# Rank-48 adapter products in a block of FFN, attention and FFN: three fp32r partial products instead of one float32 product

## The reference, cut to what is computed

```python
x = x + 0.5 * ffn(layernorm(x))        # first FFN
x = x + attention(layernorm(x))        # 32 heads, causal, 2 x 1024 rows
x = x + 0.5 * ffn(layernorm(x))        # second FFN, same weights

def ffn(x):                            # x: (2, 1024, 1024), all float32
    y = einsum('bsd,od->bso', x, weight) + bias
    seg = searchsorted(lora_start_indices, arange(2), side='right') - 1
    adapter_idx = clip(seg - 1, 0, 2)  # which of 3 adapters the batch row uses
    A, Bw = lora_A[adapter_idx], lora_B[adapter_idx]     # rank 16
    lo = (x @ A.T) @ Bw.T
    return y + where(seg > 0, lo, 0)
```

## Time and profile before

| | |
|---|---|
| median of 3 runs | 1962.72 us (1962.16 to 1965.12) |
| the profiled execution | 1964.07 us, of which 1962.1 us span |
| mean granted TensorE clock | 0.974 of 2.4 GHz |
| TensorE matmul busy | 1819.1 us, 93% |
| VectorE, ScalarE, GpSimd busy | 1230.6, 997.6, 870.1 us |
| FFN 1 | from the start to about 246 us |

### The profile page before, as it was taken

How to read it: one execution, slowest core, us unless ns; L and a number is a source line. 1 busy time by engine, 2 the same in 40 slices (tenths; PEclk the granted TensorE clock), 3 DMA queues, 4 the chain that set the end, 5 groups by cost and what they waited for, 6 DMA issues and landing times. The chain is left out here.

```text
span 1962.1 us, 44377 instructions
## 1 busy us (share of the span) xinstructions
PE 1819.1 (93%) x15472; PEld 1423.7 (73%) x15472; DVE 1230.6 (63%) x2653; ACT 997.6 (51%) x2135; POOL 870.1 (44%) x641
## 2 busy tenths in 40 slices
PE   6999968689999999999999999997699999979999
PEld 4678767667777777777777777775488888857887
DVE  5555356378889889888898888887421121125553
ACT  2211055478888888888887888885410010012110
POOL 2231110268777787787877877873000000004311
PEclk9999989899999999999999999999799999989999
DMA  6442152402221221211212212211742223224321
GB/s 224 167 167 91 60 150 71 107 23 70 65 77 50 71 77 55 83 60 55 83 60 72 66 49 83 66 67 56 261 134 88 86 96 117 65 107 158 132 86 65
DMA packets 111695, 182.45 MB, mean 93 GB/s; under 512 B 27472, under 2 KB 64464, under 8 KB 109584
## 3 DMA queue, kind: packets, MB, share of 16 engines
q1 hardware_dynamic: 111632, 181.61, 28.5%
HBM read 122.06 MB, written 59.51 MB: 93 GB/s over the span
## 5 line engine op out<-in xcount | busy, mean ns | idle before, releaser
L940 PE MATMUL psS<-keyT,q 128*128 128x512 f32 (+2 forms) x2304 | 474.3, 351 | 32.7 <-POOL q L1145 25.3
L940 PEld LDWEIGHTS psS<-keyT,q 128*128 128x128 f32 x2304 | 381.9, 190 | 127.6 <-DVE negmax L1071 41.4
L1021 ACT ACTIVATE prob<-prob,negmax 128x640 f32<-128x640 f32 (+7 forms) x512 | 391.9, 767 | 78.7 <-DVE negmax L1071 76.4
L1081 DVE STREAM_TRANSPOSE pT<-prob 128x640 f32<-128x640 f32 (+7 forms) x512 | 380.2, 762 | 66.3 <-PE psV L957 63.3
L1071 DVE CUSTOM_DVE_ANT_0 prob<-psS,mask 128x640 f32<-128x640 f32 (+7 forms) x512 | 371.9, 742 | 40.0 <-PE psS L940 26.3
L413 PE MATMUL f_psy<-f_weff,f_xT 128*128 128x512 f32 x1344 | 313.9, 393 | 0.0
L1307 PE MATMUL o_psy<-o_w,o_o 128*128 128x512 f32 x1344 | 304.8, 389 | 0.0
L1136 POOL TENSOR_TENSOR pT<-pT,cosT 64x512 f32<-64x512 f32 x128 | 164.6, 1286 | 302.6 <-ACT pT L1006 288.5
L1307 PEld LDWEIGHTS o_psy<-o_w,o_o 128*128 128x128 f32 x1344 | 252.3, 188 | 52.3
L413 PEld LDWEIGHTS f_psy<-f_weff,f_xT 128*128 128x128 f32 x1344 | 250.8, 188 | 54.0 <-issue 1.7
L957 PE MATMUL psV<-pT,val 32*64 32x512 f32 (+3 forms) x8192 | 264.8, 407 | 6.6 <-DVE pT L1081 6.2
(11 more groups left out here) (99 smaller groups left out, 1882.3 us busy)
## 6 DMA issues: line engine op xcount, KB each, us to landing
wo<-in_wo SPq DMA_DIRECT2D x16, 1024.0 KB, 5.6
pT<-row_scales SPq DMA_DIRECT2D x128, 128.0 KB, 2.8
oT<-pT SPq DMA_DIRECT2D x64, 256.0 KB, 2.4
o_in<-oT SPq DMA_DIRECT2D x32, 512.0 KB, 5.2
f_xt<-in_x SPq DMA_DIRECT2D x16, 512.0 KB, 4.1
f_w_in<-in_w SPq DMA_DIRECT2D x16, 512.0 KB, 6.9
w_sum<-f_w_in SPq DMA_DIRECT2D x16, 512.0 KB, 5.1
x<-f_xo SPq DMA_DIRECT2D x16, 512.0 KB, 3.0
```

The lines of the kernel that those rows point to most:

```text
L940: ins = nc.tensor.matmul(psS[:, slot, start + x0:start + x1], q[:, e, a, t * P:(t + 1) * P], k.keyT[:, m, b * S + x0:b * S + x1], start=(i ...
L1021: nc.scalar.activation(row, row, ACT.Exp, bias=negmax[:, n % 8:n % 8 + 1], scale=-1.0, accum_out=rowsum[:, column(n, s):column(n, s) + 1]) ...
L1081: nc.vector.transpose(pT[:, n % 2, t, 0:width], prob[:, n % RING, 0:width]).then_inc(turned, 1)
```

## The change

The adapters' A and B are packed to 48 rows and padded to `PACKED` = 64, and loaded twice, into partitions 0 to 63 and 64 to 127. `lora_a` and `lora_b` now lie in `xo`. ScalarE rounds both copies to fp32r (`gated[:, 0]` for A, `b_hi` for B), ahead of the first `root_of`. GpSimd computes `b_lo`, the rest of B, before its first piece. VectorE replaces the upper 64 rows of A by their rest (`adapters_lo`) before gate_of(0). `gate_of` writes fp32r over 128 rows. A piece's half is then two fp32r matmuls: 128 rows against `b_hi` (A hi B hi + A lo B hi), and 64 rows against `b_lo` (A hi B lo). `wanted` becomes an input of 128 x 1 that is loaded instead of set by GpSimd. GpSimd's first two `add_bias` wait for both gates, since `xo` holds the adapters until then.

```diff
+            lora_a, lora_b = xo[:, 0, :], xo[:, 1, :]
+            b_lo = c.sb("lora_b_lo", [PACKED, D], F32R)
+            b_hi = c.sb("lora_b_hi", [P, D], F32R)
+            gated = c.sb("gated", [P, B, D], F32R)
@@ sync
-                sp.dma_start(starts[:], ...to_broadcast([GATED, STARTS])).then_inc(starts_in, 16)
-                sp.dma_start(lora_a[:], a_d[:, :]).then_inc(a_in, 16)
-                sp.dma_start(lora_b[:], b_d[:, :]).then_inc(b_in, 16)
+                sp.dma_start(starts[:], ...to_broadcast([P, STARTS])).then_inc(starts_in, 16)
+                sp.dma_start(wanted[:], wanted_d[:, :]).then_inc(starts_in, 16)
+                for rows in (slice(0, PACKED), slice(PACKED, P)):
+                    sp.dma_start(lora_a[rows, :], a_d[:, :]).then_inc(a_in, 16)
+                    sp.dma_start(lora_b[rows, :], b_d[:, :]).then_inc(b_in, 16)
@@ gpsimd
+                elif w_d is not None:
+                    pool.wait_ge(gate, B)
                 nc.gpsimd.tensor_tensor(xo[:, j, :], f.xt[:, j, :], bias_half[:], ALU.add)
...
-                for a in range(ADAPTERS):
-                    nc.gpsimd.memset(wanted[32 * a:32 * a + 32, :], float(a + 2)).then_inc(numbered, 1)
+                pool.wait_ge(b_split, 1)
+                nc.gpsimd.tensor_tensor(b_lo[:], lora_b[0:PACKED, :], b_hi[0:PACKED, :].bitcast(F32),
+                                        ALU.subtract).then_inc(b_rest, 1)
+                pool.wait_ge(b_rest, 1)
             pieces_low([0])
@@ scalar
+                act.wait_ge(a_in, 32)
+                nc.scalar.activation(gated[:, 0, :], lora_a, ACT.Copy).then_inc(a_split, 1)
+                act.wait_ge(b_in, 32)
+                nc.scalar.activation(b_hi[:], lora_b, ACT.Copy).then_inc(b_split, 1)
             f.root_of(nc, act, k.eps_ln[:], 0, 0)
@@ tensor
-                    pe.wait_ge(b_in, 16)
+                    pe.wait_ge(b_split, 1)
+                    pe.wait_ge(b_rest, 1)
...
-                    ins = nc.tensor.matmul(ps_w[:, half, :], gated[:, i // DT, (i % DT) * P:(i % DT + 1) * P],
-                                           lora_b[:, half * BANK:(half + 1) * BANK], start=True, stop=True)
+                    nc.tensor.matmul(ps_w[:, half, :], gated[:, i // DT, x], b_hi[:, y], start=True, stop=False)
+                    ins = nc.tensor.matmul(ps_w[:, half, :], gated[0:PACKED, i // DT, x], b_lo[:, y], start=False, stop=True)
@@ vector
+            def adapters_lo():
+                dve.wait_ge(a_split, 1)
+                nc.vector.tensor_tensor(lora_a[PACKED:P, :], lora_a[PACKED:P, :],
+                                        gated[PACKED:P, 0, :].bitcast(F32), ALU.subtract).then_inc(a_rest, 1)
+                dve.wait_ge(a_rest, 1)
...
             f.normalise(nc, dve, 0, 0)
             if w_d is not None:
+                adapters_lo()
                 gate_of(0)
             make_pieces([0])
```

More of the change, by code:

```diff
@@ L33 @@
 STARTS = 4
-GATED = 32 * ADAPTERS
+PACKED = 64
 QT = S // P
@@ L214, in ffn_phase @@
             ps_w = c.ps(tag + "ps_w", [P, 2, BANK])
[L215 to L223, removed]
+            lora_a, lora_b = xo[:, 0, :], xo[:, 1, :]
+            b_lo = c.sb("lora_b_lo", [PACKED, D], F32R)
+            b_hi = c.sb("lora_b_hi", [P, D], F32R)
+            gated = c.sb("gated", [P, B, D], F32R)
+            starts = c.sb("starts", [P, STARTS], I32)
+            startf = c.sb("startf", [P, STARTS])
+            hit = c.sb("hit", [P, B, STARTS])
+            count = c.sb("count", [P, B])
+            wanted = c.sb("wanted", [P, 1])
+            chosen = c.sb("chosen", [P, B])
             starts_in, a_in, b_in = c.sem("starts_in"), c.sem("lora_a_in"), c.sem("lora_b_in")
-            numbered, chain, gate = c.sem("numbered"), c.sem("chain"), c.sem("gate")
+            chain, gate = c.sem("chain"), c.sem("gate")
+            a_split, b_split, a_rest, b_rest = c.sem("lora_a_hi"), c.sem("lora_b_hi"), c.sem("lora_a_lo"), c.sem("lora_b_lo")
         bias_in, halved = c.sem(tag + "bias_in"), c.sem(tag + "halved")
@@ L270, in _ @@
             if w_d is not None:
-                a_d, b_d, starts_d = adapters
-                sp.dma_start(starts[:], starts_d.rearrange("(a n) -> a n", a=1).to_broadcast([GATED, STARTS])).then_inc(starts_in, 16)
-                sp.dma_start(lora_a[:], a_d[:, :]).then_inc(a_in, 16)
-                sp.dma_start(lora_b[:], b_d[:, :]).then_inc(b_in, 16)
+                a_d, b_d, starts_d, wanted_d = adapters
+                sp.dma_start(starts[:], starts_d.rearrange("(a n) -> a n", a=1).to_broadcast([P, STARTS])).then_inc(starts_in, 16)
+                sp.dma_start(wanted[:], wanted_d[:, :]).then_inc(starts_in, 16)
+                for rows in (slice(0, PACKED), slice(PACKED, P)):
+                    sp.dma_start(lora_a[rows, :], a_d[:, :]).then_inc(a_in, 16)
+                    sp.dma_start(lora_b[rows, :], b_d[:, :]).then_inc(b_in, 16)
             load_w(0)
@@ L341, in pieces_hi @@
                     nc.scalar.activation(weff[:, i // DT, HI, i % DT, :], w_in[:, i % SLOTS, :], ACT.Copy).then_inc(w_hi, 1)
+            if w_d is not None:
+                act.wait_ge(a_in, 32)
+                nc.scalar.activation(gated[:, 0, :], lora_a, ACT.Copy).then_inc(a_split, 1)
+                act.wait_ge(b_in, 32)
+                nc.scalar.activation(b_hi[:], lora_b, ACT.Copy).then_inc(b_split, 1)
             f.root_of(nc, act, k.eps_ln[:], 0, 0)
@@ L373, in outer_products @@
                 for half in range(2):
-                    ins = nc.tensor.matmul(ps_w[:, half, :], gated[:, i // DT, (i % DT) * P:(i % DT + 1) * P],
-                                           lora_b[:, half * BANK:(half + 1) * BANK], start=True, stop=True)
+                    x, y = slice((i % DT) * P, (i % DT + 1) * P), slice(half * BANK, (half + 1) * BANK)
+                    nc.tensor.matmul(ps_w[:, half, :], gated[:, i // DT, x], b_hi[:, y], start=True, stop=False)
+                    ins = nc.tensor.matmul(ps_w[:, half, :], gated[0:PACKED, i // DT, x], b_lo[:, y], start=False, stop=True)
                 ins.then_inc(outer, 1)
@@ L437, in link @@
                     dve.wait_ge(chain, next(links))
-                dve.wait_ge(starts_in, 16)
-                dve.wait_ge(numbered, ADAPTERS)
+                dve.wait_ge(starts_in, 32)
                 link(nc.vector.tensor_copy(startf[:], starts[:]))
@@ L445, in choose @@
                     link(nc.vector.tensor_scalar(chosen[:, b:b + 1], count[:, b:b + 1], wanted[:, 0:1], None, ALU.is_equal))
+            def adapters_lo():
[3 more added lines that the diff above has]
+                dve.wait_ge(a_rest, 1)
             def gate_of(b):
-                dve.wait_ge(a_in, 16)
-                nc.vector.tensor_scalar(gated[:, b, :], lora_a[:], chosen[:, b:b + 1], None, ALU.mult).then_inc(gate, 1)
+                nc.vector.tensor_scalar(gated[:, b, :], lora_a, chosen[:, b:b + 1], None, ALU.mult).then_inc(gate, 1)
             def results(n, j):
@@ L1315, in output_steps, with macaron_block @@
     steady(eng, step, NT, 1, 1, start=0)
-def macaron_block(nc, x, wa, lnw, wn, wpe, wv, wo, cos, sin, cosT, sinT, w, bias, lora_a, lora_b, starts, out):
+def macaron_block(nc, x, wa, lnw, wn, wpe, wv, wo, cos, sin, cosT, sinT, w, bias, lora_a, lora_b, starts, wanted, out):
     x1_d = nc.dram_tensor("x1", (T, D), F32).ap()
@@ L1334, in macaron_block @@
         constants_phase(nc, k)
-        ffn_phase(nc, "f1_", k, x, x1_d, bias, sum_d, w, (lora_a, lora_b, starts))
+        ffn_phase(nc, "f1_", k, x, x1_d, bias, sum_d, w, (lora_a, lora_b, starts, wanted))
         with ExitStack() as inner:
@@ L1388 @@
     blank = _np.zeros((NOPE, S), _np.float32)
-    blank_rows = _np.zeros((ADAPTERS, 32 - RANK, D), _np.float32)
+    blank_rows = _np.zeros((PACKED - ADAPTERS * RANK, D), _np.float32)
+    wanted = _np.concatenate([_np.repeat(_np.arange(2.0, ADAPTERS + 2.0), RANK), _np.zeros(PACKED - ADAPTERS * RANK)])
     data = {
@@ L1406 @@
         "bias": get("L0_ffn_bias"),
-        "lora_a": _np.concatenate([get("L0_ffn_lora_A"), blank_rows], 1).reshape(GATED, D),
-        "lora_b": _np.concatenate([get("L0_ffn_lora_B").transpose(0, 2, 1), blank_rows], 1).reshape(GATED, D),
+        "lora_a": _np.concatenate([get("L0_ffn_lora_A").reshape(ADAPTERS * RANK, D), blank_rows], 0),
+        "lora_b": _np.concatenate([get("L0_ffn_lora_B").transpose(0, 2, 1).reshape(ADAPTERS * RANK, D), blank_rows], 0),
         "starts": get("L0_ffn_lora_start_indices"),
+        "wanted": _np.concatenate([wanted, wanted]).astype(_np.float32).reshape(P, 1),
     }
```

## The result

The changed kernel takes 1970.93 us (median of 8 runs, 1968.05 to 1974.52), the one before 1963.28 us (8 runs). The ratio is 1.0038, with a 95% interval of 1.0027 to 1.0049: **slower by 0.4%**, where 0.15% faster was forecast and the range ended at 1964.0. The profiled execution took 1970.85 us, its span 1968.8 us, against 1964.07 and 1962.1: +6.7 us in the span. The medians are 7.65 us apart, so about 1 us of their difference is not in these two traces.

A forecast was written before the change was run, and what follows sets the result against it. In FFN 1, latencies bound the start, VectorE and x loads the stretch to about 45 us, TensorE mostly the later steps. Start +4.0 and body -6.8 gave -2.8 us, a median of 1959.9 us; range 1956.2 to 1964.0.

The forecast's parts named there:

- the price of the new products: FFN 1 outer products: four fp32r products a piece at 0.227 us, 0.91 against 1.72 us, saving 0.81 where TensorE bounds.
- another distance than 0.227: Sign the prediction is wrong: products over 64 rows standing at a distance other than 0.227 us.
- rival 4: New products aren't cheaper than float32 ones; the body gains nothing, the start stays: 1966.7 us, chance 0.04.
- the body: FFN 1 after its start: savings of 7.4 us less a stall of 0.6, a gain of 6.8 us.
- the start: FFN 1 up to the add of piece 0: adapter landing, copies and `b_lo` move it from 15.92 to 19.9, +4.0 us.
- the turn of tile 5: Steps 2 to 4: x tiles come late by their own chain, one stall of 0.6 us, bounds 0 and 1.5.
- The tables: ScalarE at the start: a 1.28 us table load between copy of B and root is hidden by `b_lo`, cost 0.
- Pieces 9 and 10: FFN 1: piece 9's serial chain saves 0.9 us; piece 10, where TensorE is the bound, saves 0.81 us.
- other stretches: FFN 1 to about 60 us, VectorE-paced then TensorE-bound: a low clock in more of them would make the prediction wrong.
- Piece 3: Early FFN 1: gains about 0.8 us at 32.34, loses it at 42.14 where VectorE waits for tile 3.
- The wait for tile 3's DMA: At 42.14 us tile 3's statistics still wait for their load, which hangs on GpSimd's bias add; 2.10 us before.
- Rivals 1 to 3: Cheaper start, 1957.2 us (0.25); dearer start, about 1962.7 us (0.18); B landing late, slower (0.08).

The follow-up runs named there:

- the experiment: Changed kernel with one Sqrt of a constant on ScalarE ahead of the adapters' copies, so the second table load falls away: 1969.66 us, a single run.
- both edits: Changed kernel with the second product over 128 rows and tile 0's root ahead of ScalarE's copies: 1961.38 us against 1964.45, ratio 0.9982.

## Why the prediction was wrong, point by point

**The step that failed is the price of the new products.** The text gave bounds of 0.11 and 0.227 us for the 64-row product "since the 128-row products are the nearest rows", and took 0.227. Measured it was 0.43, and its neighbour of 128 rows 0.43 as well; the text had named another distance than 0.227 as a sign of being wrong. Both bounds were prices of a product in a run of its own kind. The trace of before had no change between 64 and 128 rows inside FFN 1, so the price of the edge had no row, and above 0.227 there was no bound. A bound from the other side was at hand: 0.19 us for a load with nothing beside it and 0.24 us behind it make 0.43, the price that rival 4 supposed without a mechanism. With four edges of 0.2 us a piece, 0.8 us are lost, which is the 0.81 that was to be saved. Rival 4 (chance 0.04) gave 1966.7 us. In the traces the body was to gain 6.8 us and lost 0.9, and the start was to cost 4.0 and cost 5.57; together that is the whole way from -2.8 to +6.5.

**With that term set right, the rest of the sum is near.** The version with 128 rows is the change as the prediction priced it. Its median is 3.1 us below the kernel before (1961.42 against 1964.52), where 2.8 was predicted. The parts in its trace: step 12.69 us for 12.7, start +4.69 (its first add at 20.61) for +4.0, the rest of FFN 1 -6.3 (its next phase begins at 245.23, against 246.80) for -6.8, the turn of tile 5 short by 0.73 us for 0.6. These parts add up to -1.6 us, and so do the spans (1960.5 against 1962.1). The other 1.5 us of the median are not in these two traces, so that 3.1 comes so near to 2.8 is in part luck.

**The start**: direction and order were right, the size was +5.57 for +4.0. The copy of B began at 12.23 us for 12.0. `b_lo` and the normalise fell as described: end at 16.25 for 16.1, 0.55 us behind `b_lo`. The gate ended at 18.3 and the first product began at 18.44 for 18.0. The four products up to the add took 3.05 us for 1.9, which is the failed step again, on the slow array: 0.72 us each for 0.45. (The granted clock reads 1.00 in the windows from 16 to 30 us, but loads of 0.28 us at a distance of 0.72 are what piece 9 shows where it reads 0.50.) That is 1.15 of the 1.57 us that the start was off.

**The tables**: a second load did come, 1.28 us at 13.30, and was hidden as the text said; the experiment shows the cover. The estimate from the Trainium skill, "ScalarE: Activation LUTs", section "What ACT_TABLE_LOAD costs", of 2.66 us for a switch had the root end later than `b_lo`. It didn't come about: from the end of the copy, 13.29, to the begin of the root at 14.60 it is 1.31 us.

**Pieces 9 and 10**: forecast as a gain of 0.9 at piece 9 beside the one of piece 10; after, they lost 0.9 us together. One part is the distance of 0.43. The other is that the clock stood at its lower level for some 7 us instead of 3.5. That part doesn't seem to be the change's, as far as single executions can tell. The version with the table load moved has the same work in this stretch; there the loads show the lower level from 71.9 to 75.3 us only, and the next phase begins 4.7 us later than before with a start of +5.0, so the body cost -0.3 instead of +0.9. With both edits and `b_lo` on GpSimd the clock stayed at 2.4 GHz from 60 to 80 us. What decides it in an execution is open; the prediction had named the clock, but for other stretches.

**Piece 3** gained its 0.8 us with 128 rows (add at 36.24, +3.90 where the start stood at +4.69), and lost it sooner than the text had it, at the rest of that piece:

```profile
38.59 3.53 DVE L247 TENSOR_TENSOR f_weff<-f_w_in,f_weff 128x1024 fp32r<-128x1024 f32 x1 [1.13 <-ACT f_weff L349]
38.59 2.43 POOL L318 TENSOR_TENSOR f_xo<-f_xt,f_bias_half 128x1024 f32<-128x1024 f32 x1
```

Both start at once, VectorE sits out GpSimd's whole 2.43 us and takes 3.53 us for 2.68. The wait for tile 3's DMA behind it stayed as said (2.30 us there, 1.93 after, 2.10 before). Rivals 1 to 3 didn't occur: the adapters landed where the forecast had them, and most of what the start cost beyond it was the products.

## What to carry to other kernels

A price taken from a trace holds for an instruction among neighbours like those it had there. Before giving a new matmul the distance of an old one, look at whether its contraction has the same extent as the ones around it; here 64 rows between 128-row products cost 0.2 us at every border, while the 64-row products saved nothing over 128-row ones, and filling them up to 96 or 128 rows was free. And when a step is put ahead of another on an engine's queue, as the adapters' copies ahead of the root, ask what is already there and ready: moving the root back won 2.5 us at the first product, of which 1.7 were left at the end of FFN 1.

## What the runs showed of the hardware that was not expected

- Neighbouring products over 64 and over 128 rows: the load of the second one's stationary operand isn't hidden behind the first. For fp32r it is 0.43 us for 0.23 at 2.4 GHz and 0.72 for 0.43 at 1.2 GHz, and the gap shows in both directions (0.36 and 0.37 us in the order 128, 128, 64, 64). For float32 outer products of 64 rows a step took 13.91 us for 13.50. Between 96 and 128 rows, and between 64 and 64, it is hidden.
- VectorE's `b_lo` of 128 x 1024 took 1.22 us, GpSimd's 2.34 and 2.42, and beside the latter a VectorE instruction of 0.75 us took 2.71 us. Here, what GpSimd took over from VectorE was dear, since VectorE had something to do meanwhile.
- The gate with an fp32r output over 128 rows took 0.75 us, as much as with a float32 output over 96 (0.74).
